# Rotation in four wide GpSimd operations, and contexts split a step earlier, in a windowed attention kernel

## The reference

```python
q = _apply_rope(proj(Wq, bq))       # 16 heads of 64
k = _apply_rope(proj(Wk, bk))
v = proj(Wv, bv)
# _apply_rope(x): x * cos + concatenate([-x2, x1]) * sin, x1 and x2 the halves of the 64
scores = jnp.einsum('bhnqd,bhnkd->bhnqk', qb, kcat) * scale   # own block of 128 keys and the one before
attn = jax.nn.softmax(jnp.where(valid, scores, -1e30), axis=-1)
ctx = jnp.einsum('bhnqk,bhnkd->bhnqd', attn, vcat)
out = merged @ Wo.T + bo
```

## Time and profile before

| | |
|---|---|
| time, median of 3 runs (lowest, highest) | 1629.46 us (1627.92, 1631.04) |
| profiled execution, first to last instruction | 1627.8 us |
| PE busy | 1505.6 us, 92% |
| DVE busy | 1401.5 us, 86% |
| ACT busy | 1318.2 us, 81% |
| POOL busy | 1031.1 us, 63% |
| PE, DVE, ACT, POOL busy in 600 to 800 us | 190.5, 183.5, 165.5, 139.7 of 200 us |
| mean granted TensorE clock | 0.983 |

### The profile page before, as it was taken

How to read it: one execution, slowest core, us unless ns; L and a number is a source line. 1 busy time by engine, 2 the same in 40 slices (tenths; PEclk the granted TensorE clock), 3 DMA queues, 4 the chain that set the end, 5 groups by cost and what they waited for, 6 DMA issues and landing times. The chain is left out here.

```text
span 1627.8 us, 46635 instructions
## 1 busy us (share of the span) xinstructions
PE 1505.6 (92%) x16930; PEld 1152.3 (71%) x16930; DVE 1401.5 (86%) x3881; ACT 1318.2 (81%) x2394; POOL 1031.1 (63%) x788
## 2 busy tenths in 40 slices
PE   5999978899999999999999999999999999869998
PEld 4888745576766777676767666766777677658887
DVE  5999678899999899999998998999899989857885
ACT  5999657888878888878887887878888878849996
POOL 4665267677667777767677776667777767513443
PEclk8999999999999999999999999999999999979999
DMA  5233246989998989899998999998989899962331
GB/s 210 91 124 107 78 85 120 175 152 191 157 184 162 179 157 181 168 176 176 163 179 157 179 164 175 157 182 163 175 162 182 154 174 154 176 159 69 109 106 75
DMA packets 721530, 247.90 MB, mean 152 GB/s; under 512 B 687380, under 2 KB 706072, under 8 KB 721304
## 3 DMA queue, kind: packets, MB, share of 16 engines
q1 hardware_dynamic: 720600, 244.53, 77.4%
q10 hardware_dynamic: 704, 0.40, 0.1%
HBM read 47.73 MB, written 25.17 MB: 45 GB/s over the span
## 5 line engine op out<-in xcount | busy, mean ns | idle before, releaser
L1450 ACT ACTIVATE at_prob<-at_prob,at_top 128x256 f32<-128x256 f32 (+1 forms) x1024 | 428.5, 490 | 42.1 <-DVE at_top L1262 39.0
L1262 DVE CUSTOM_DVE_ANT_0 at_prob<-banks,at_masks,pre_s_scale 128x256 f32<-128x256 f32 (+1 forms) x1024 | 420.3, 471 | 19.7 <-PE banks L1703 6.7
L1585 PE MATMUL banks<-at_xt,pre_w_h 128*128 128x512 f16 x1024 | 297.5, 383 | 22.6 <-ACT at_v_l L1478 21.9
L1274 DVE TENSOR_TENSOR at_halves<-at_prob,at_halves 128x1024 f16<-128x1024 f32 (+1 forms) x256 | 315.5, 1233 | 1.2 <-ACT at_halves L1459 1.2
L1703 PE MATMUL banks<-at_kt,at_qt 32*128 32x256 f32 (+1 forms) x4096 | 251.6, 382 | 38.8 <-POOL at_qt L1183 19.5
L1459 ACT ACTIVATE at_halves<-at_prob 128x1024 f16<-128x1024 f32 (+1 forms) x256 | 263.4, 1029 | 6.1
L1703 PEld LDWEIGHTS banks<-at_kt,at_qt 32*128 32x128 f32 x4096 | 197.4, 186 | 99.8 <-issue 95.5
L1204 POOL TENSOR_TENSOR at_c_halves<-at_ctx,at_c_halves 128x1024 f16<-128x1024 f32 x64 | 136.7, 2136 | 178.0 <-DVE at_halves L1274 172.4
L1173 POOL TENSOR_TENSOR at_kt<-at_k_by 128x512 f32<-128x512 f32 x128 | 163.2, 1275 | 95.6 <-DVE at_halves L1274 95.4
L1183 POOL TENSOR_TENSOR at_qt<-at_q_by 128x512 f32<-128x512 f32 x128 | 223.0, 1761 | 0.0
L1163 POOL TENSOR_TENSOR at_q_by<-at_q_first,at_tables 128x512 f32<-128x512 f32 x128 | 163.2, 1275 | 83.5 <-DVE at_halves L1274 83.5
(11 more groups left out here) (128 smaller groups left out, 3280.4 us busy)
## 6 DMA issues: line engine op xcount, KB each, us to landing
f_x<-in_x SPq DMA_DIRECT2D x16, 512.0 KB, 3.7
x_after_ffn<-f_x SPq DMA_DIRECT2D x16, 512.0 KB, 2.6
at_x_ln<-x_after_ffn SPq DMA_DIRECT2D x16, 512.0 KB, 3.5
at_x_res<-x_after_ffn SPq DMA_DIRECT2D x64, 128.0 KB, 3.0
x_after_attention<-at_x_res SPq DMA_DIRECT2D x64, 128.0 KB, 2.7
f_x<-x_after_attention SPq DMA_DIRECT2D x16, 512.0 KB, 4.6
out_x<-f_x SPq DMA_DIRECT2D x16, 512.0 KB, 3.0
at_tables<-in_cos SPq DMA_DIRECT2D x16, 256.0 KB, 4.0
```

What stands on the lines that cost most here:

```text
L1262: last = nc.vector.tensor_tensor_reduce(out=prob[:, n % 2, h, low:2 * P], in0=s_ps[:, h, n % 2 * 2 * P + low:(n % 2 + 1) * 2 * P], in1=mas ...
L1274: nc.vector.tensor_tensor(parts[:, 1, :, :], prob[:, n % 2, :, keys_from(t, b):2 * P], parts[:, 0, :, :], ALU.subtract).then_inc(p_low, 1)
L1450: last = nc.scalar.activation(at, at, ACT.Exp, bias=top[:, n % 2, h:h + 1], scale=-1.0)
L1585: last = nc.tensor.matmul(pr_ps[:, half, :].rearrange("p (b t) -> p b t", b=SB), w[wp][:, k, at:at + P], xt[:, r, xp, :, k, :], start=n == ...
```

## The change

- **Rotation.** The two products of a first half become one POOL operation of 128x1024 that reads the copy twice by a broadcast; DVE's product by sin is made negative (with a negated bias, a reversed subtraction), so that both sums are additions and one POOL operation of 128x1024 adds them. Four POOL operations stand per step for rotation where eight stood, and two semaphores where there were four.
- **Contexts.** `context_low` and `turn_context` take the context of step t - 1 instead of t - 2, at the end of the step, behind `after_p_low(t, 2)`. On ACT `context_high(t - 1)` stands ahead of `p_high_of(t, 3)`.
- **Order.** On POOL keys are finished at the start of the step and queries after `p_low_of(t, 1)`, and the inverse deviation comes behind the queries. On ACT `carry_keys` is taken for step t, not t - 1, behind `p_high_of(t, 3)`, and `normalize` and `x_high_of` come behind it. On DVE `p_low_of(t, 2)` goes ahead of `shift_of`, and `p_low_of(t, 3)` ahead of `x_low_of`.

```diff
@@ Prepared.vector
+            for n in range(2):
+                nc.vector.tensor_scalar(self.neg_bias[:, n, :], self.bias[:, n, :], w_up[:, n:n + 1], -1.0, ALU.mult,
+                                        ALU.mult)
@@ sync, at_step
             turn_p(t - 1, 3)
-            turn_context(t - 2)
             turn_p(t, 0)
...
             turn_p(t, 2)
+            turn_context(t - 1)
@@ gpsimd
-                nc.gpsimd.tensor_tensor(k_by[:, n, :], k_first[:, :], tables[:, r, n // 3, :],
-                                        ALU.mult).then_inc(k_made[n], 1)
+                nc.gpsimd.tensor_tensor(k_by[:, 0:2, :], k_first[:, :].unsqueeze(1).broadcast_to([P, 2, SB * P]),
+                                        tables[:, r, :, :], ALU.mult).then_inc(k_first_made, 1)
...
-                nc.gpsimd.tensor_tensor(kt[:, half, own(t, 0):own(t, 0) + SB, :].rearrange("p s t -> p (s t)"),
-                                        k_by[:, 2 * half, :], k_by[:, 2 * half + 1, :],
-                                        (ALU.subtract, ALU.add)[half]).then_inc(k_roped[half], 1)
+                nc.gpsimd.tensor_tensor(kt[:, :, own(t, 0):own(t, 0) + SB, :].rearrange("p h s t -> p h (s t)"),
+                                        k_by[:, 0:2, :], k_by[:, 2:4, :], ALU.add).then_inc(k_roped, 1)
...
             after_p_low(t - 1, 3)
-            context_low(t - 2)
-            key_product(t + 1, 0)
-            key_product(t + 1, 3)
+            key_products(t + 1)
+            key(t + 1)
             after_p_low(t, 0)
-            key(t + 1, 1)
-            query_product(t + 1, 0)
+            query_products(t + 1)
             after_p_low(t, 1)
-            query_product(t + 1, 3)
+            query(t + 1)
             if g == 3 and S > -2:
                 inverse_std(S + 2)
-            key(t + 1, 0)
-            query(t + 1, 1)
-            query(t + 1, 0)
+            after_p_low(t, 2)
+            context_low(t - 1)
@@ vector
-                nc.vector.scalar_tensor_tensor(k_by[:, n, :], pr_ps[:, 1, :], bias[:, 1, 2 * g + 1:2 * g + 2],
-                                               tables[:, r, n % 2, :], ALU.add, ALU.mult).then_inc(k_made[n], 1)
+                by = (neg_bias, bias)[n][:, 1, 2 * g + 1:2 * g + 2]
+                nc.vector.scalar_tensor_tensor(k_by[:, 2 + n, :], pr_ps[:, 1, :], by, tables[:, r, 1 - n, :],
+                                               (ALU.subtract, ALU.add)[n], ALU.mult,
+                                               reverse0=n == 0).then_inc(k_second_made, 1)
...
+            p_low_of(t, 2)
             if g == 3 and S > -2:
                 shift_of(S + 2)
-            p_low_of(t, 2)
             residual(t - 5)
             context(t, 0)
+            key_product(t + 2, 0)
             key_product(t + 2, 1)
-            key_product(t + 2, 2)
+            p_low_of(t, 3)
             if g == 3 and S > -2:
                 x_low_of(S + 2)
-            p_low_of(t, 3)
@@ scalar
             query_copy(t + 1)
-            carry_keys(t - 1)
...
+            context_high(t - 1)
+            p_high_of(t, 3)
+            carry_keys(t)
             if g == 3 and S > -2:
                 normalize(S + 2)
-            if g == 3 and S > -2:
                 x_high_of(S + 2)
-            p_high_of(t, 3)
-            context_high(t - 1)
             key_copy(t + 2)
@@ tensor, scores
-                for half in range(2):
-                    pe.wait_ge(k_roped[half], t + 1)
-                    pe.wait_ge(q_roped[half], t + 1)
+                pe.wait_ge(k_roped, t + 1)
+                pe.wait_ge(q_roped, t + 1)
```

More of the change, by code:

```diff
@@ L963, in attention_stage @@
     q_copied = sem("q_copied")
-    k_made = [sem(f"k_product{n}") for n in range(4)]
-    q_made = [sem(f"q_product{n}") for n in range(4)]
-    k_roped = [sem("k_first_roped"), sem("k_second_roped")]
-    q_roped = [sem("q_first_roped"), sem("q_second_roped")]
+    k_first_made = sem("k_first_made")
+    q_first_made = sem("q_first_made")
+    k_second_made = sem("k_second_made")
+    q_second_made = sem("q_second_made")
+    k_roped = sem("k_roped")
+    q_roped = sem("q_roped")
     k_carried = sem("k_carried")
@@ L1097, in load_tables @@
             if big(S):
-                for n in range(4):
-                    need(q_made[n], NG * (S - 1))
-                    need(k_made[n], NG * (S - 1))
+                for products, each in ((k_first_made, 1), (q_first_made, 1), (k_second_made, 2), (q_second_made, 2)):
+                    need(products, each * NG * (S - 1))
                 at = SB * P * (S % SPB)
@@ L1161, in query_product, with key, query @@
                 pool.wait_ge(q_copied, t + 1)
-                need(q_roped[n // 2], t)
-                nc.gpsimd.tensor_tensor(q_by[:, n, :], q_first[:, :], tables[:, r, n // 3, :],
-                                        ALU.mult).then_inc(q_made[n], 1)
-        def key(t, half):
+                need(q_roped, t)
+                nc.gpsimd.tensor_tensor(q_by[:, 0:2, :], q_first[:, :].unsqueeze(1).broadcast_to([P, 2, SB * P]),
+                                        tables[:, r, :, :], ALU.mult).then_inc(q_first_made, 1)
+        def key(t):
             if step(t):
-                pool.wait_ge(k_made[2 * half], t + 1)
-                pool.wait_ge(k_made[2 * half + 1], t + 1)
+                pool.wait_ge(k_first_made, t + 1)
+                pool.wait_ge(k_second_made, 2 * t + 2)
                 need(s_done, 2 * t - 2)
                 need(k_carried, carried(t - 2))
-                nc.gpsimd.tensor_tensor(kt[:, half, own(t, 0):own(t, 0) + SB, :].rearrange("p s t -> p (s t)"),
-                                        k_by[:, 2 * half, :], k_by[:, 2 * half + 1, :],
-                                        (ALU.subtract, ALU.add)[half]).then_inc(k_roped[half], 1)
-        def query(t, half):
+                nc.gpsimd.tensor_tensor(kt[:, :, own(t, 0):own(t, 0) + SB, :].rearrange("p h s t -> p h (s t)"),
+                                        k_by[:, 0:2, :], k_by[:, 2:4, :], ALU.add).then_inc(k_roped, 1)
+        def query(t):
             if step(t):
-                pool.wait_ge(q_made[2 * half], t + 1)
-                pool.wait_ge(q_made[2 * half + 1], t + 1)
+                pool.wait_ge(q_first_made, t + 1)
+                pool.wait_ge(q_second_made, 2 * t + 2)
                 need(s_done, 2 * t - 2)
-                nc.gpsimd.tensor_tensor(qt[:, t % 2, half, :], q_by[:, 2 * half, :], q_by[:, 2 * half + 1, :],
-                                        (ALU.subtract, ALU.add)[half]).then_inc(q_roped[half], 1)
+                nc.gpsimd.tensor_tensor(qt[:, t % 2, :, :], q_by[:, 0:2, :], q_by[:, 2:4, :],
+                                        ALU.add).then_inc(q_roped, 1)
         def inverse_std(S):
@@ L1391, in at_step @@
             tops(t, 1)
-            query_product(t + 1, 2)
+            query_product(t + 1, 1)
             context(t - 1, 1)
-            query_product(t + 1, 1)
+            query_product(t + 1, 0)
             p_low_of(t, 0)
@@ L1504, in key_copy @@
                 act.wait_ge(k_done[0], t + 1)
-                need(k_made[0], t)
-                need(k_made[3], t)
+                need(k_first_made, t)
                 nc.scalar.activation(k_first[:, :], pr_ps[:, 0, :], ACT.Identity,
@@ L1514, in query_copy @@
                 act.wait_ge(q_done[0], t + 1)
-                need(q_made[0], t)
-                need(q_made[3], t)
+                need(q_first_made, t)
                 nc.scalar.activation(q_first[:, :], pr_ps[:, 0, :], ACT.Identity,
```

34 lines of the change are left out of this document (17 added, 17 removed).

## The result

| | before | after |
|---|---|---|
| time, median (lowest, highest), us | 1628.69 (1627.2, 1631.04), 4 runs | 1705.43 (1704.32, 1706.71), 4 runs |
| profiled execution, first to last instruction, us | 1627.8 | 1702.4 |
| PE, DVE, ACT, POOL busy in 400 to 1300 us | 853.6, 818.6, 743.4, 633.4 | 822.5, 808.6, 704.4, 537.3 |
| key products on DVE, from the 4th of the attention to the 64th, us | 254.33 to 1394.71 | 265.71 to 1469.51 |

The change makes the kernel slower: the ratio is 1.047, 95% interval [1.0458, 1.0484], +77 us. The forecast was 1657 us with a range up to 1676, so the side was right and the size was not. The last row of the table splits the difference of the two profiled executions (74.6 us): **+11.4 us** before the fourth step's products, **+63.4 us** in the 60 steps that follow (1203.80 against 1140.38), **-0.2 us** behind them.

What follows compares the result with a forecast made beforehand. No engine was saturated; a loop over several engines was taken to set step length. Terms 17.7 + 14.0 - 2 - 2.3 = +27.4 us on 1627.8 gave 1655.2, plus 1.7 for the median: 1657 us, range 1616 to 1676.

Steps and rivals of the forecast that it cites:

- The operation must fit in the gaps between DVE's remainders: POOL's wide rotation operations: query products would end at 798.6 against a remainder at 798.44, as today; costed at nothing.
- The loop was forecast at +31.7 us (17.7 + 14.0): Attention steps: +17.7 us for `context_low` meeting DVE's last remainder, +14.0 us for the later `x_low_of`.
- `context_low` beside the last remainder: End of step: DVE's last remainder meets POOL's context split and loses 0.5 us in 35 steps, +17.7 us.
- PE's freed wait pays for it in 14 of 49 steps: Steps without layer norm where PE sets the pace: its freed 0.53 us wait for queries offsets the collision, 0.
- `x_low_of` behind the last remainder: Layer-norm super-blocks: next maxima start 1.07 us later in 11, 0.76 in 3, +14.0 us; POOL's key products not under it.
- POOL's operations, 2.4 us: Rotation on POOL: each 128x1024 operation takes 2.4 us, bounds 2.13 and 2.50.
- Rival 3: POOL's 1024-column operations take 2.8 us, key operations reach into the first remainder; +25, 1682 us; chance 0.12.
- Two operations on 8 columns at the start: 0: DVE at the start: two operations on 8 columns, from the negated product, cost 0.
- Shift behind a remainder, inverse deviation behind the queries: 0: DVE's shift no longer meets POOL, the inverse deviation may; DVE's 0.87 us idle before the keys covers both, 0.
- Outputs and tail, -2 and -2.3 us: Outputs at a super-block's start wait less, about -2 us; last `context_high` no longer waits 2.29 us, -2.3 us.
- Rival 1: PE sets the pace and its freed wait comes back whole, -33 us, 1594 us; chance with part cases 0.17.
- Its case with half of the steps: Part case where half of the steps are PE's: terms -8, +8 and the ends, about 1615 us.

Runs made afterwards that it cites:

- run 1: Changed kernel with PE projecting the second bank of keys ahead of the next scores, so ACT's key copy comes earlier; 1678.61 us, ratio 1.0296.
- run 5: Kernel before with only the contexts moved (`context_low`, `turn_context`, `context_high`), rotation still in 128x512 operations; 1680.6 us, ratio 1.0322.
- run 2: Changed kernel with `context_low` on one block of four (128x256) in all steps but the first; 1704.15 us, ratio 1.0451.
- run 3: Changed kernel with keys ahead of the scores on PE and `context_low` on one block of four, together; 1670.4 us, ratio 1.0244.
- run 7: run 3 with the layer norm's order of before on ACT and DVE; 1663.3 us, ratio 1.0213.
- run 4: Changed kernel with all orders of before on every engine, leaving the wide rotation operations and negated product alone; 1644.6 us, ratio 1.0095.
- run 8: Changed kernel with POOL's sums, DVE's last remainder, ACT's f16 copy and layer norm reordered to take both collisions away; 1671.93 us, ratio 1.0264.
- run 6: run 4 with DVE's `shift_of` behind the third remainder, as in the changed kernel; 1643.02 us, ratio 1.0098.

## Why the prediction was wrong

- **"The operation must fit in the gaps between DVE's remainders"**: this is the step that failed. I followed it for the query products, which do fit, and costed the whole at nothing. The key sum does not fit: its start hangs on ACT's key copy, and 2 x 2.36 us behind it reach 0.89 us into the first remainder. The row that would have told was at hand: before, POOL's key products were the first thing behind a `context_low`, and taking that one away leaves POOL waiting for the copy, a wait which I never placed. Run 1, without this collision, has 60 steps that are 30.9 us shorter. The loop was forecast at +31.7 us (17.7 + 14.0) and came to +63.4, so this term is about all of what the loop lacked. That run 1 then stands at +32.5, beside the forecast, is partly luck, as the next two points say.
- **`context_low` beside the last remainder**: mechanism, place and price per step were right (2.16 us after the values for 2.1, 0.55 us for 0.5). The count was not. The idea that PE's freed wait pays for it in 14 of 49 steps did not hold: the remainder is long in 44 of 45 steps, and DVE's wait for the keys grew at the same time from 0.87 to 1.26 us. +17.7 us stays unproven as a size: run 5 shows 50.6 us for the contexts' place, with a deeper collision (0.87 us) and a late f16 copy, while runs 2 and 3, which take this collision away, are 0.2 and 1.3 us shorter in the 60 steps than the changed kernel and run 1.
- **`x_low_of` behind the last remainder**: DVE's idle before it went from 0.47 to 0.98 us, and run 7 puts 5 to 7 us on it where I had +14.0. The first remainder behind that step keeps to 1.22 us, so there the collision that was not forecast is missing. And POOL did start its key products under `x_low_of`, which I had ruled out: they take 2.67 us in 13 steps, held to its end.
- **POOL's operations, 2.4 us**: right (2.36). The mean of 2433 ns for the key products contains the 14 that `x_low_of` held up. The estimate of 2.3 us from the Trainium skill, page "GPSIMD Engine Reference", section "Performance versus the Vector engine", comes to 2.2 us, with 2.6 cycles per element and the 1.2 GHz of that page's table. Rival 3, longer operations of 2.8 us, gives 1682 us and named the place, the two key operations reaching into the first remainder; it had the wrong condition, for they reach into it at 2.36 us.
- **"Two operations on 8 columns at the start: 0" and "Shift behind a remainder, inverse deviation behind the queries: 0"**: in the loop the shift is indeed free (0.15 us), but at the start 11.4 us are lost, of which I had none.
- **Outputs and tail, -2 and -2.3 us**: the end moved by 0.2 us. ACT's last `context_high` starts at 1518.93, 183.5 us before the end, where before it was 1444.32, also 183.5 us before it: the wait of 2.29 us is gone (it starts right behind other work), and nothing came of it. What ends the kernel was not followed further.
- **Rival 1**, PE sets the pace: its sign was wrong. PE's wait for the queries went, and no time came back. Its case with half of the steps is also added up wrongly: -8, +8 and the ends (-4.3) give about 1625 us, not 1615.

Summed from the traces: 11.4 at the start, 63.4 in the loop, -0.2 at the end, 74.6 us of the profiled execution. That the collisions make the loop longer is shown by run 1 for the first remainder (up to the unknown price of PE's order) and, for the last, by run 5 against run 4 (with ACT's order mixed in). How far the steps would return if both collisions went and nothing else changed stays open: runs 2, 3 and 8 each brought the next wait (the other collision, late scores, a late transfer with a new collision).

## What to carry to other kernels

A wait of one engine that another operation used to fill is part of the schedule: before an operation is moved away, place the wait that it leaves behind, and follow what stands behind it to the next operation of the engine it can collide with. Merging operations on such an engine saves its time but can make a collision longer, up to nearly the whole of the merged one (2.1 of 2.36 us in run 4). Two collisions in a loop do not add: taking the first away may only deepen the second, so test them together and apart.

## What the runs showed of the hardware

In these rows the exclusion is by whole operations, and the one that starts second pays. In four pairs of rows above a POOL operation runs first and DVE's remainder ends 1.08 or 1.09 us behind its end (851.77 and 852.86; 858.77 and 859.85; 860.08 and 861.16 in run 2; 834.72 and 835.80 in run 5), as if its own 1.22 us began 0.13 us before that end, whether it was started 0.7 or 1.45 us ahead of that end. It is the same throughout: in the trace of the changed kernel all 97 held remainders of 1024 columns end 1.07 to 1.10 us behind the end of the POOL operation that was running when they started. The POOL operation keeps its 2.13 or 2.36 us. The other way round it is the same: in run 6 POOL's sum takes 3.10 us behind a remainder. It holds for small operations too: a cast of 128x256, with one input, took 2.38 us instead of 0.29, and a shift of four columns 2.31 instead of 0.17. The maxima and the products of DVE, which read PSUM, keep their 0.48 and 0.75 us while POOL is busy.

The Trainium skill, page "SBUF — State Buffer", section "SBUF: two separate sides", calls the shared port pair "an exclusive lock, not a bandwidth split", held for the whole instruction by the one that starts first, against DVE operations with two SBUF inputs or in a 2-port performance mode. The rows agree for the operations with two SBUF inputs (the remainders and the shift). The cast reads one tile, and the scaling one tile and a factor per row; whether they ran in such a mode no row shows.

A longer POOL operation therefore holds DVE longer. By the 0.13 us above, one half of the rotation's sum (1.27 us) could hold a remainder for 1.1 us at most, an estimate; whole (2.36 us) it held one for 1.3 us in run 2 and a shift for 2.1 us in run 4, with no more work done.
